# An attention and expert kernel on one core: the last batch's heads load early into the weight ring, the row table is made first, and ScalarE reads levels early

## The reference

```python
x = x + attn(layernorm(x), W_DKV, W_UK, W_UV, W_UQ, W_O)
x = x + ffn(layernorm(x), Wr, temp, W1, b1, W2, b2)

# attn: 16 heads of 16 columns, keys and values through a latent of 64
c_kv = x @ W_DKV
k, v, q = c_kv @ W_UK, c_kv @ W_UV, x @ W_UQ
probs = softmax(where(causal, q k^T / 4, -inf))
ctx = probs v;  return ctx @ W_O

# ffn: 8 experts of 512, two per token
logits = x @ Wr / temp;  topw, topi = top_k(logits, 2);  topw = softmax(topw)
for e in range(8):
    a, g = split(x @ W1[e] + b1[e])
    out += ((a * silu(g)) @ W2[e] + b2[e]) * weight_of(e)
```

## Time and profile before

| | us |
|---|---|
| median of 3 executions | 1049.57 (1048.76 to 1050.04) |
| the profiled execution | 1049.65 |
| its span, first to last instruction | 1047.8 |
| PE busy, of the span | 958.1 (91%) |
| DVE busy | 782.6 (75%) |
| ACT busy | 555.0 (53%) |
| POOL busy | 508.1 (48%) |
| mean granted clock of PE | 0.94 of 2.4 GHz |

### The profile page before, as it was taken

How to read it: one execution, slowest core, us unless ns; L and a number is a source line. 1 busy time by engine, 2 the same in 40 slices (tenths; PEclk the granted TensorE clock), 3 DMA queues, 4 the chain that set the end, 5 groups by cost and what they waited for, 6 DMA issues and landing times.

```text
span 1047.8 us, 21901 instructions
## 1 busy us (share of the span) xinstructions
PE 958.1 (91%) x5804; PEld 574.1 (55%) x5805; DVE 782.6 (75%) x2291; ACT 555.0 (53%) x1202; POOL 508.1 (48%) x972
## 2 busy tenths in 40 slices
PE   4999899999999999999989956299999999999993
PEld 2444243333333333333345546288888888888883
DVE  3675999999999999999966556466766666676762
ACT  1555067777777777777763535143433334434431
POOL 5555536666666666666633745543322323233232
PEclk9999589999999999999997966599999999999998
DMA  3688966485867867644456588753555375333332
GB/s 98 215 266 213 234 137 153 93 257 99 257 153 216 250 156 209 150 90 89 89 149 184 188 217 275 224 161 52 140 134 131 50 210 136 55 50 56 54 51 35
DMA packets 107729, 156.53 MB, mean 149 GB/s; under 512 B 26944, under 2 KB 82240, under 8 KB 105088
## 3 DMA queue, kind: packets, MB, share of 16 engines
q1 hardware_dynamic: 83696, 128.03, 45.8%
q0 software_dynamic: 13296, 17.77, 9.8%
q10 hardware_dynamic: 10656, 9.78, 3.5%
HBM read 90.46 MB, written 64.69 MB: 148 GB/s over the span
## 4 chain that ended last, share of the span: by engine, by line
PE 78%; DVE 8%; DMA 5%; ACT 3%; issue 2%; POOL 1%; ACTq 1%; SPq 0%; DVEq 0%; POOLq 0%
PE bank L860 13%; PE bank L881 13%; PE bank L842 13%; PE bank L2020 6%; PE bank L2022 6%; PE bank L2021 6%; PE bank L2050 3%; PE bank L2052 3%; PE bank L2051 3%; PE bank L2034 3%; PE bank L1632 2%; DMA e_rows<-slot_rows 2%; DVE a_xn L314 2%; PE a_ckv L363 2%; PE bank L1996 1%
## 5 line engine op out<-in xcount | busy, mean ns | idle before, releaser
L816 ACT ACTIVATE b_prob<-bank 128x512 f32<-128x512 f32 (+3 forms) x768 | 311.9, 507 | 79.7 <-PE bank L860 78.9
L842 PE MATMUL bank<-b_k_st,b_q_st 96*128 96x512 bf16 (+3 forms) x768 | 255.6, 346 | 5.8 <-DVE b_neg_max L770 1.7
L770 DVE CUSTOM_DVE_ANT_0 bank<-bank,b_mask_max 128x256 f32<-128x256 f32 (+3 forms) x512 | 241.6, 510 | 22.2 <-PE bank L842 22.0
L860 PE MATMUL bank<-b_q_st,b_k_st 99*128 99x512 bf16 (+3 forms) x768 | 242.9, 334 | 4.0 <-ACT b_prob L816 2.0
L726 POOL TENSOR_SCALAR_AFFINE_SELECT b_prob<-b_prob 128x128 f32<-128x128 f32 x512 | 147.0, 300 | 188.5 <-ACT b_prob L816 184.2
L1846 POOL DMA_INDIRECT out_dram<-e_y,e_token x71 | 110.5, 1557 | 238.6 <-issue 158.0
L773 DVE TENSOR_REDUCE b_neg_max<-bank 128x1 f32<-128x512 f32 x256 | 175.8, 687 | 13.4 <-PE bank L842 11.2
L881 PE MATMUL bank<-b_prob,b_v_aug 128*32 128x512 f32 (+3 forms) x1536 | 146.3, 500 | 0.0
L842 PEld LDWEIGHTS bank<-b_k_st,b_q_st 96*128 96x128 bf16 x768 | 75.9, 99 | 109.3 <-DVE b_neg_max L770 52.1
L860 PEld LDWEIGHTS bank<-b_q_st,b_k_st 99*128 99x128 bf16 x768 | 74.8, 99 | 106.3 <-ACT b_prob L816 79.1
L2020 PE MATMUL bank<-w_ring,e_rowsT_hi 128*128 x284 | 125.3, 441 | 3.5 <-DVE e_rowsT_lo L1871 2.2
(11 more groups left out here) (203 smaller groups left out, 1470.7 us busy)
## 6 DMA issues: line engine op xcount, KB each, us to landing
w_parts<-w_ring SPq DMA_DIRECT2D x10, 1536.0 KB, 7.3
w_ring<-w_parts SPq DMA_DIRECT2D x10, 1024.0 KB, 7.6
e_rows<-slot_rows ACTq DMA_DIRECT2D x74, 129.0 KB, 2.1
w_raw<-in_L_ffn_W SPq DMA_DIRECT2D x8, 1024.0 KB, 5.2
ctx_cols<-b_ctx_out SPq DMA_DIRECT2D x16, 512.0 KB
...
```

Source lines behind the costliest of these rows:

```text
L770: nc.vector.tensor_tensor_reduce(scores, scores, mask_max[:, HALF - width:HALF], -1.0, -MASKED, ALU.add, ALU.min, to).then_inc(max_done, 1)
L816: nc.scalar.activation(prob[n % NP][:, 0:width], prob_ps[n % NS][:, 0:width], ACT.Exp, scale=SCALE).then_inc(prob_ok, 1)
L842: nc.tensor.matmul(out[:, 0:width], q_st[g % RING][0:STACK, h, i * P:(i + 1) * P], k_st[g % RING][0:STACK, h, half * HALF:half * HALF + wi ...
L860: nc.tensor.matmul(prob_ps[n % NS][:, 0:width], k_st[g % RING][0:MAXROWS, h, j * P:(j + 1) * P], q_st[g % RING][0:MAXROWS, h, q0:q0 + widt ...
```

## The change

Four things change. **Heads of batch 3** go to a place of their own, the first 8 KB per partition of the ring's fourth slot (`w_raw`), so that their load waits for nothing; it is issued second, right after `load_den(3)`, and no longer behind the scale. SP waits for the scale of batch 3 to land before it stores batch 2's result. **scale_heads(3)** stands before slots(1) on DVE. **The tables:** DVE computes the start rows right after the tile's group number and announces them with a semaphore of their own, `tile_row_ok`; the sum over 666 elements is taken on one partition into the bytes of `m_fresh`; experts and fresh flags follow and set `tables_ok`. **ACT** waits for the levels (`level_ok`, set after slots(2)), reads the first three, waits for `tile_row_ok`, and does load 0, load 1, `rows_high(0)`, load 2.

```diff
--- before.py
+++ after.py
@@ -966,6 +966,7 @@
         self.wo = freed("c_wo", [P, DC, D])
         self.xnT.append(freed("c_xnT1", [P, 2, DC, P]))
         self.heads = freed("c_heads", [P, DC, SEQ])
+        self.last_heads = weights.raw[:, W_STAGES, 0, 0:DC * SEQ].rearrange("p (c n) -> p c n", c=DC)
         self.x2 = [freed("c_x2_0", [P, BT, D])]
         self.scale = freed("c_scale", [P, DC, SEQ])
         self.x2.append(freed("c_x2_1", [P, BT, D]))
@@ -990,6 +991,7 @@
         self.inv_den = early("c_inv_den", [P, P])
         self.tile_level = early.beside("c_den_in1", "m_tile_level", [1, TABLE], I32)
         self.tile_f = early.beside("c_den_in0", "r_tile_f", [P, TABLE])
+        self.jumped = self.fresh[:].bitcast(F32)
         self.stats = early("c_stats", [P, BT, 6])
         self.mean_var = early("c_mv", [P, BT, 2])
         self.var_eps = early("c_var_eps", [P, BT])
@@ -1075,6 +1077,8 @@
         self.pad_slot_ok = sem("r_pad_slot_ok")
         self.spare_st = sem("r_spare_st")
         self.tables_ok = sem("r_tables_ok")
+        self.tile_row_ok = sem("r_tile_row_ok")
+        self.level_ok = sem("r_level_ok")
 
     def follow(self, turn_bank, prob_sc_ok, prob_ok, pv_ok, max_done, rows_ok, v_aug_ok, acc_out, ctx_st):
 
@@ -1109,11 +1113,14 @@
             sp.dma_start(self.scale[:, c, :], of.unsqueeze(1).to_broadcast([P // HD, HD, SEQ])).then_inc(
                 self.scale_in_ok, 16)
 
+    def heads_of(self, b):
+        return self.heads[:] if b < BATCH - 1 else self.last_heads
+
     def load_heads(self, sp, b):
-        if b:
+        if 0 < b < BATCH - 1:
             sp.wait_ge(self.proj_ok, b * PAIRS)
         context = self.dram["ctx"].rearrange("g (q s) n -> s (g q) n", s=2)[0]
-        sp.dma_start(self.heads[:], context[b * D:(b + 1) * D, :].rearrange("(c p) n -> p c n", p=P)).then_inc(
+        sp.dma_start(self.heads_of(b), context[b * D:(b + 1) * D, :].rearrange("(c p) n -> p c n", p=P)).then_inc(
             self.heads_in_ok, 16)
 
     def load_x(self, sp, b):
@@ -1170,10 +1177,11 @@
         nc, dram, pad_row = self.nc, self.dram, self.pad_row
 
         self.load_den(sp, 3)
+        self.load_heads(sp, 3)
         self.store_inverse(sp, 3)
         self.load_scale(sp, 3)
-        self.load_heads(sp, 3)
         self.load_x(sp, 3)
+        sp.wait_ge(self.scale_in_ok, 16 * DC * BATCH)
         self.store_x2(sp, 2)
 
         sp.wait_ge(self.pad_row_ok, 1)
@@ -1310,11 +1318,12 @@
 
         def scale_heads(b):
 
+            heads = self.heads_of(b)
             dve.wait_ge(self.heads_in_ok, 16 * (b + 1))
             dve.wait_ge(self.scale_in_ok, 16 * DC * (b + 1))
             for k in range(SCALES):
                 half = slice(k // DC * CHUNK, (k // DC + 1) * CHUNK)
-                nc.vector.tensor_tensor(self.heads[:, k % DC, half], self.heads[:, k % DC, half],
+                nc.vector.tensor_tensor(heads[:, k % DC, half], heads[:, k % DC, half],
                                         self.scale[:, k % DC, half], ALU.mult).then_inc(self.heads_ok, 1)
 
         def residual(b):
@@ -1460,7 +1469,8 @@
                                     ALU.mult, ALU.add)
             then(nc.vector.tensor_scalar(level[:], self.tile_index[0:1, :], full[0:1, :], 1.0, ALU.is_ge, ALU.add))
             nc.vector.scalar_tensor_tensor(out=self.tile_level[:], in0=self.tile_index[0:1, :],
-                                           scalar=self.full_two[0:1, 0:1], in1=level[:], op0=ALU.is_ge, op1=ALU.add)
+                                           scalar=self.full_two[0:1, 0:1], in1=level[:], op0=ALU.is_ge,
+                                           op1=ALU.add).then_inc(self.level_ok, 1)
 
         def pad_slots():
             then(nc.vector.tensor_tensor(self.pad_slot_f[:], self.region[:], start[:], ALU.add))
@@ -1485,6 +1495,13 @@
                                          self.tiles_end[:].unsqueeze(1).to_broadcast([P, TABLE, SEGMENTS]),
                                          ALU.is_ge))
             then(nc.vector.tensor_reduce(tile_f[:], passed[:], AX.X, ALU.add))
+            then(nc.vector.tensor_tensor(passed[:], passed[:],
+                                         self.jump[:].unsqueeze(1).to_broadcast([P, TABLE, SEGMENTS]),
+                                         ALU.mult))
+            then(nc.vector.tensor_reduce(self.jumped, passed[0:1], AX.X, ALU.add))
+            then(nc.vector.tensor_tensor(same[:], self.row_of_tile[:], self.jumped, ALU.add))
+            then(nc.vector.tensor_scalar(self.tile_row[:], same[:], float(EXPERTS * REGION), None, ALU.min))
+            dve.sem_inc(self.tile_row_ok, 1)
 
             then(nc.vector.tensor_scalar(same[:], tile_f[0:1, :], 0.0, 2.0, ALU.is_equal, ALU.mult))
             then(nc.vector.scalar_tensor_tensor(out=same[:], in0=tile_f[0:1, :], scalar=float(SEGMENTS - 1),
@@ -1499,14 +1516,7 @@
                                                 op1=ALU.mult))
             nc.vector.tensor_scalar(same[:, 0:1], tile_f[0:1, 0:1], 0.0, None, ALU.mult)
             then(nc.vector.tensor_scalar(same[:, 1:TABLE], same[:, 1:TABLE], 1.0, None, ALU.mult))
-            then(nc.vector.tensor_scalar(self.fresh[:], same[:], -16.0, 16.0, ALU.mult, ALU.add))
-            then(nc.vector.tensor_tensor(passed[:], passed[:],
-                                         self.jump[:].unsqueeze(1).to_broadcast([P, TABLE, SEGMENTS]),
-                                         ALU.mult))
-            then(nc.vector.tensor_reduce(tile_f[:], passed[:], AX.X, ALU.add))
-            then(nc.vector.tensor_tensor(same[:], self.row_of_tile[:], tile_f[0:1, :], ALU.add))
-            nc.vector.tensor_scalar(self.tile_row[:], same[:], float(EXPERTS * REGION), None,
-                                    ALU.min).then_inc(self.tables_ok, 1)
+            nc.vector.tensor_scalar(self.fresh[:], same[:], -16.0, 16.0, ALU.mult, ALU.add).then_inc(self.tables_ok, 1)
             dve.wait_ge(self.tables_ok, 1)
 
         dve.wait_ge(self.const_ok, 8)
@@ -1527,9 +1537,9 @@
         residual(2)
         moments(2)
         choose(1)
+        scale_heads(3)
         slots(1)
         filled_by_two()
-        scale_heads(3)
         shift(2)
         residual(3)
         moments(3)
@@ -1630,7 +1640,7 @@
         for i in range(2):
             for c in range(DC):
                 last = self.nc.tensor.matmul(self.project_bank(b, t)[:, i * D:(i + 1) * D],
-                                             self.heads[:, c, (2 * t + i) * P:(2 * t + i + 1) * P],
+                                             self.heads_of(b)[:, c, (2 * t + i) * P:(2 * t + i + 1) * P],
                                              self.wo[:, c, :], start=(c == 0), stop=(c == DC - 1))
         last.then_inc(self.proj_ok, 1)
 
@@ -1928,11 +1938,13 @@
 
     @block.scalar
     def _(act):
-        def load(n, c):
+        def level_of(n):
+            return act.value_load(entry(route.tile_level, n), min_val=1, max_val=3)
+
+        def load(n, c, level=None):
 
             act.wait_ge(y_ok, n + 1)
-            level = act.value_load(entry(route.tile_level, n), min_val=1, max_val=3)
-            act.wait_ge(landed, level)
+            act.wait_ge(landed, level_of(n) if level is None else level)
             act.sem_inc(load_turn, 1)
             row = act.value_load(entry(tile_row, n), min_val=0, max_val=EXPERTS * REGION)
             act.dma_start(rows[c % B][:], dram["rows"][bass.ds(row, P), :]).then_inc(rows_ok[c % B], 16)
@@ -1975,12 +1987,15 @@
             if value is None or n < SLOT_TILES:
                 silu(n, c)
 
-        act.wait_ge(route.tables_ok, 1)
+        act.wait_ge(route.level_ok, 1)
+        levels = [level_of(n) for n in range(AHEAD)]
         route.rows_written(act, BATCH - 2)
         route.tokens_written(act)
+        act.wait_ge(route.tile_row_ok, 1)
         for n in range(AHEAD):
-            load(n, n)
-        rows_high(0, 0)
+            load(n, n, levels[n])
+            if n == 1:
+                rows_high(0, 0)
         steps(act, step)
         for n in range(SLOT_TILES, TABLE):
             act.wait_ge(rows_ok[n % B], (n // B + 1) * 16)
@@ -2067,8 +2082,8 @@
 
         pe.sem_inc(a_ok, 1)
         pe.sem_inc(y_ps_ok, 1)
+        rows_turned(0, 0)
         pe.wait_ge(route.tables_ok, 1)
-        rows_turned(0, 0)
         steps(pe, step)
```

## The result

The change is slower. The changed kernel took 1052.01 us (median of 21 runs, 1049.20 to 1056.58), the kernel before 1049.65 us on the same chip (21 runs, 1047.28 to 1051.92). The ratio is 1.0031, with a 95% interval of 1.0021 to 1.0041. The prediction was 1045.6 us, in a range of 1041.5 to 1049.5, with 0.06 on slower.

A forecast was written before the change was run, and what follows sets the result against it. PE binds most of the run (78% of the wait chain), so only the experts' start at 673.92 us could move. Terms 1.7 + 1.85 + 0.86 - 1.2 + 0.9 gave 4.1 us; forecast 1045.6 us, range 1041.5 to 1049.5.

The forecast's parts named there:

- step 1: Early heads of batch 3: the scale lands by 615.6 us and DVE's multiplication gains 2.4 us against 618.01.
- X: Time at which batch 3's scale has landed and its multiplication can start: 615.6 us, bounds 612.7 and 617.
- The skill's rule: DMA engine count for the scale's broadcast load: 8 engines, an estimated 4.5 us; the forecast took 11 us instead.
- The quick scale: Rival, chance 0.18: x hardly disturbs the scale's load, X is 612.7, time 1040.5 to 1042.7 us.
- step 2: slots(1) behind the multiplication: POOL's scatters bind and take 0.7 us; normalise(3) at 633.7, gain 1.7 us.
- my fourth rival: Slower, chance 0.06: DVE's scale wait ahead of slots(1) delays scatters, normalise(3) and biases; 1052 us at X = 622.
- step 3: DVE's tables: the experts and fresh flags block moves behind the start rows, gain 1.85 us.
- step 4: ACT before the first tile load: the level's read ahead of load 0 is gone, gain 0.86 us.
- step 5: Bias loads, begun at 644.9, end at 667.7 and slow the first tile load: cost 1.2 us, bounds 0 and 3.8.
- step 6: ACT's first tile copy no longer waits for load 2's issue: gain 0.9 us.
- Behind the start: Expert stage: the end follows the experts' start one for one, with the stage as long as before.

The follow-up runs named there:

- e5: Kernel before, with only DVE's multiplication of batch 3's heads moved ahead of slots(1) and the count of filled slots: 1055.85 us, 1.0050 of before.
- e7: Kernel before plus the change's tables and ScalarE half, with ScalarE's first six tile loads not waiting for free buffers: 1046.12 us, 0.9955 of before.
- e4: Kernel before plus only the change's second half (tables and ScalarE), free-buffer wait kept: 1049.34 us, 0.9995 of before.
- e14: The same kernel as e7, timed again on another chip: 1070.23 us, 0.9978 of before.
- e3: Changed kernel, with ScalarE's first six tile loads not waiting for free buffers and the first copy waiting for the tables: 1053.87 us, 1.0038 of before.
- e2: Changed kernel, with the ring's load behind the level-3 semaphore and held until PE has begun tiles 12 and 14: 1052.71 us, 1.0026 of before.
- e13: Changed kernel, with the ring's load right behind the level-3 semaphore, not held further: 1077.19 us, 1.0039 of before.
- e1: Changed kernel, with DVE's old order (heads multiplied behind slots(1) and filled_by_two), heads still loaded early: 1050.85 us, 1.0009 of before.
- e6: Kernel before, with only batch 3's heads loaded early and SP's wait for the scale: 1050.62 us, 1.0001 of before.
- e9: Changed kernel, with DVE's old order and no free-buffer wait for the first tile loads, heads issued ahead of the inverse's store: 1066.41 us, 0.9970 of before.
- e8: e7 plus a Silu over a dead buffer ahead of the tile loads and the first Silu ahead of the copy: 1048.08 us, 0.9978 of before.
- e10: e9 with the early heads issued right behind the inverse's store instead of ahead of it: 1065.75 us, 0.9969 of before.

## Why the prediction was wrong

**The multiplication's start (step 1)** was the step that failed first. I had the store landing at 603.1, right after the heads, and the scale in after 11 us: X = 615.6. Counted from E, the store was issued 1.0 us later than I had it (E+9.3), took 4.20 us instead of 2.7, and the multiplication began 13.1 us behind the scale's issue instead of 12.4. That the wait for heads would give way to one for the scale was right. But all three terms came out late, some 3.1 us together, and the multiplication is 0.7 us later where I had 2.4 us of gain. A second fault was mine alone: I compared absolute times although attention's end moves by 1.6 us from one execution to the next; X = 617.1 looks like the edge of my bounds (612.7 and 617), but they are E+20.6 and E+24.9, and it is E+26.6.

**The skill's rule** (the Trainium skill, DMA: Bandwidth & Descriptors, "Why a DMA increments its semaphore by 16 and not by 1"), weighed there, would have had the scale in after some 4.5 us by an estimate from its page. The trace has 12.42 us beside x. The 8 engines that it counts fit the trace of the kernel before: in 569 to 576 us, where batch 2's scale loads nearly alone, the DMA share is 0.50, half of the 16. The rate does not: these moved 125 GB/s together. The quick scale fell with it.

**slots(1) behind the multiplication (step 2)** was right as a mechanism and is what makes the change slower. normalise(3) is released by a scatter 18.5 us behind the multiplication's start (I had 18.1). But its sign hung on X. With no gain at X, the 10.4 us by which the scatters move are pure cost: 1.8 us at normalise(3), and the biases, the pad rows and the ring 6 to 10 us later. I took for SyncE's queue that only the biases matter. The kernel is slower by the mechanism of my fourth rival, DVE's wait ahead of slots(1). I put 0.06 on it and its point of decision at X = 619.7, because I made the gain of the other steps its cushion. By that sum the late X alone would have left 1.0 us of gain; the cushion was not there, for the two reasons below (`y_ok` and the stage behind the start). e5 shows it alone: 1.0050.

**The tables (step 3) and ScalarE's reads (step 4)** were worth 2.7 us in my sum. From normalise(3) to the end of the start rows it is 28.66 us (before 30.75), as said. The first load is 32.0 us behind normalise(3), where I had 30.0. The step left out is `y_ok`. I wrote that PE's wait for `tables_ok` has slack, and did not ask what else DVE gives only at the end of that code. e7 against e4 prices it at 2.9 us at the first product and 4 thousandths in the ratios, on two chips; with e14 in e7's place, on a third, it is 1.7 thousandths. In the changed kernel, where the biases are late, taking it out gained nothing (e3).

**The biases (step 5)** began 22.6 us behind the first scatter, where I had 22.8, though at E+55.5 and not at E+52.8, since X was late. The last of them landed at about 669.5. The first load, late as it was, met only their last 2 us and landed in 2.73 us. In e3, where it came 2.1 us earlier from E, it met 5 us of them and took 5.1 us. So the mechanism was right and its size (4.2) too small by 0.9; in the changed kernel it stood behind a later wait.

**The early copy (step 6)** came 0.04 us behind PE's transposes (670.41 + 0.69 to 671.14), a gain of 0.9 us as said. That, and a landing 0.2 us shorter, is why the first product is only 0.1 us later although the load is 1.2 us later.

**The sum, term by term, at the first product.** normalise(3): -1.8 us (forecast +1.7). From there to the load: +0.7 (+2.7). The tile's landing: +0.2 (-1.2). The early copy: +0.9 (+0.9). Together they give nothing (-0.1 us in the table), where the forecast had +4.1; the 2.9 us behind the start come on top.

**Behind the start** I let the end follow the start one for one. It does not. Tile 4's load fell behind the ring's because the ring had moved 5.8 us and the loads hadn't; that one tile cost 4.4 us in the profiled execution. I had looked only at what precedes the first tile. Taking the collision away (e2, e13) did not bring the time back, so it is a form that the loss takes and was not shown to be its cause. Such losses also sit elsewhere: e1's profiled execution has no wait of PE near 690, but one of 2.31 us at 755, behind a tile load of 9.53. How the scatters, biases and ring that come 6 to 10 us later lengthen the expert stage stays open; that the move on DVE does it is shown.

How the parts add up, in thousandths: DVE's order +5.0, early heads +0.1, tables and ScalarE -0.5, sum +4.6 against +3.1 measured, each part with an interval of about 1.6, on two chips. They agree within those.

## What to carry to other kernels

When a consumer is moved ahead of other work on its engine, first ask which of its inputs lands last after the move; if that input gets no earlier, the move only puts its wait in front of everything queued behind. When a producer's output is computed earlier, list every semaphore that its consumer waits for, credits among them, and where in the producer's code each is given: the last one sets the time. And count times from the last event that the change cannot touch.

## What the runs showed of the chip

- A small store (64 KB) issued behind 1 MB of heads on the same queue is held by it: 4.2 to 5.2 us in six traces (the change, e1, e2, e3, e6, e9), against 1.6 to 2.2 in the six looked at that issue the heads behind it (before, e4, e5, e7, e8, e10).
- A tile load of 129 KB takes 2.1 us in the median. Issued 0.7 to 2.4 us behind the first of the four loads that bring the ring's 3 MB, it took 7.4 to 10.8 us in seven traces (the change, e1 to e5, e8), although it is on another engine's queue. PE stood 0.9 to 3.9 us for such a load in four of them (the change, e3, e5, e8). In the kernel before, such a load stood 3.7 us behind the ring's and took 6.8 us, and PE did not wait for it.
- An earlier start does not always start faster: in e4 the clock rose 5 us sooner than before, 3 of them counted from E, and fell again behind a wait of 1.96 us.
- The same kernel before took 1049.91 and 1050.13 us on the chips of the first two groups and 1068.71 and 1071.72 us on those of the last two. The traces of those have waits for something that the profile doesn't know, in this same stretch of straight code; in e10's view of waits from 592 to 720 (engine and product, releaser, us, times, longest):

```profile
ACT c_xnT L1595 <- remote: 11.8, 2, 8.4
...
ACT e_hiddenT_hi L1972 <- remote: 4.4, 1, 4.4
...
DVE e_y L1920 <- remote: 3.6, 1, 3.6
```

That view has no such row in any of the ten traces of the kernel before, the change and e1 to e8. What they are stays open; they lie where the change works, so a ratio from these chips says less beside one from the first two.

The fastest kernel of the study is e7: the change's second half without the wait for free buffers, 0.9955 and 0.9978 of before on two chips.
